# A decoder layer on one core: the first two and last three pipeline steps written out by hand, new loop orders, five idle products

## The chip, the cores and the metric

The kernel runs on 1 core of one Trainium2 chip. The metric is the device time of one execution in microseconds (us). The engines are TensorE (PE; its weight loads, PEld, overlap its products), VectorE (DVE), ScalarE (ACT), GpSimd (POOL) and SyncE (SP), which here only issues transfers (DMA). Each engine takes its own instructions strictly in the order in which they were written, and waits on semaphores for the others.

## The reference

For 32 batches of 112 tokens of width 256: a self attention without projections whose probabilities under 0.01 are cut out ("vacuum") and come back as a term with `W`, then a layer norm; a cross attention with 16 heads of 16 on 375 context rows with a mask, then a layer norm; a mixture of 8 experts of which the router takes 2 for each token, then a layer norm. Cut to what matters:

```
scores = x @ x.T / 16;  probs = softmax(scores)
vac = where(probs < 0.01, probs, 0);  sparse = where(probs < 0.01, 0, probs)
x1 = layernorm(x + (sparse / (sparse.sum() + 1e-9)) @ x + 0.01 * (vac.sum() broadcast) @ W.T)
q, k, v = x1 @ Wq + bq, ctx @ Wk + bk, ctx @ Wv + bv          # 16 heads of 16
attn = softmax(where(mask, -1e15, q @ k.T / 4));  x2 = layernorm(x1 + (attn @ v) @ Wo + bo)
p, i = top_k(softmax(x2 @ Wr), 2);  out = layernorm(x2 + sum_k p_k * (x2 @ Wi[i_k]) @ Wo[i_k])
```

## The kernel before

Each batch `b` goes through a software pipeline. One iteration `it` of a long unrolled loop works on several batches at a stage each: `Sc(it+3)` starts the self attention, `PT`, `att`, `x1T_`, `K0`, `K1` are for batch `it+2`, `V0`, `V1` for `it+1`, `scores` and `V2` for `it`, the second half of the attention (`oT`, `aT`, `Wo`) for `it-1`, and the experts for `it-2` and `it-3`. The loop runs for `it` from -5 to 35 (`FIRST`, `LAST`), and `at(b, step)` writes a step only where `b` is one of the 32 batches. So in the first and last iterations the steps that exist keep the order that the loop has for the full ones. A step writes its waits and its instruction; each engine has a loop of its own with its own order of steps.

- Self attention of a batch: `Sc` (TensorE), `self_max`, `self_nmax` (VectorE), `self_exponent` (ScalarE), `rsum`, `self_p`, `sparse`, `vacuum` (VectorE), `PT` (transpose), `sparseT` (ScalarE), `att`, `y1`, `stats1`, `mom1` (VectorE), `var1`, `rstd1` (GpSimd), `normalize_x1` (VectorE, L965), `x1T_`, `ax1T`, `qT`.
- Queries and keys are held as high and low parts and are laid by DMA into stacks of 97 partitions: `high_queries_out` and `low_queries_out` write them to memory, `stack_queries` (3 transfers a batch) reads them back, `stack_keys` moves the keys (4 pairs of 3 transfers a batch). The 97th partition of `k_stack` holds ones, which GpSimd writes once for each of 3 buffers (`fill_ones`, L495); that of `q_stack` takes the negated maxima (`neg_max_to_stack`).
- Cross attention: `scores(b, n)`, n = 0 to 15 (TensorE, L1259, 2 banks by turns), each followed by `head(b, n)` on VectorE (L861), which finds the maximum; `mx0` after head 7 and `mx1` after head 15 transpose the maxima (L1403, L1408). Then 12 blocks: ScalarE lays the mask into a bank (`lay_mask`; `lay_last` on VectorE for the last batch, L949), TensorE adds the scores (`score_block`, L1277), ScalarE takes the exponent (`exponent`, L595). `weigh_values` (L1293) multiplies by V in two octets, `o_sb`, `oT`, `rden`, `o_norm`, `aT`, `attnT`, `attn_rest`, `Wo`, `y2` and the second norm follow.
- Experts: `expert_product(e)` multiplies each expert's two matrices once in the opening (L1444), `high_expert` and `low_expert` split the result. The tokens are cut anew into 28 tiles of 128; a batch whose number is a multiple of 8 ends no tile. For a tile: `lg` (router), `cross`, `gate_max`, `gate_exp`, ... `gate`, four mixtures `m0` to `m3` (L1472, 6 products of 512 columns each) and eight steps `expert(t, e)` on VectorE (L1091), in the order of e, two for each mixture; then `stats3`, `mom3`, `var3`, `rstd3`, `normalize_out`, `store`.

The TensorE results of all but the score products share three banks G0, G1, G2; the list `USES` gives the order of their users, and `free` waits for the user before.

Of the kernel before, what the change touches and what calls it, by code (L numbers as in the profile page):

```python
# [49 lines left out]
PRODUCT_PLACE = (0, 1, 2, 4, 3, 5, 6, 7)  # L50
# [8 lines left out]
USES = [("m3", -3, "G2"), ("E6", -1, "G1"), ("x2T", -2, "G1"), ("PT", 2, "G0"), ("lg", -2, "G1"),  # L59
# [5 lines left out]
RELEASED = {"x2T": "x2_lo", "PT": "sparseT", "lg": "gate_max", "mx0": "nmaxT0", "V2": "v2", "Sc": "self_exp", "att": "y1", "V1": "v1", "V0": "v0", "aT": "attn_lo", "Wo": "y2", "K0": "k_lo0", "x1T": "ax1T", "K1": "k_lo1", "qT": "q1"}  # L65
FIRST, LAST = -5, BATCH + 3
# [7 lines left out]
         "o_sb", "oT", "rden", "o_norm", "aT", "attnT", "attn_lo", "Wo", "y2",  # L74
         "stats2", "mom2", "var2", "rstd2", "x2", "x2T", "x2_hi", "x2_lo", "lg",
         "cross", "gate_max", "gate_exp", "gate_r", "gate_p", "top_p", "top_i", "top_f", "gate_a",
         "gate", "m0", "m1", "m2", "m3", "stats3", "mom3", "var3", "rstd3",
         "out")
# [56 lines left out]
def decoder_layer(nc, x, x_T, context_T, mask, attn_w_T, wq, bq, wk, bk, wv, bv, wo, bo, wr, wi_T, wout,  # L135
                  consts, q_scratch, out):
    ctx = ExitStack()
    with ctx:  # L138
# [180 lines left out]
        def _(sp):  # L319
# [44 lines left out]
            def high_queries_out(b):  # L364
                sp.wait_ge(done["q_hi1"], b + 1)
                settle(sp)
                sp.dma_start(q_scratch[b % 2][0], q_hi[:, :, :, :].rearrange("p h c q -> p (h c q)").bitcast(fp32))\
                  .then_inc(q_hi_out[b % 2], 16)

            def low_queries_out(b):  # L370
                sp.wait_ge(done["q_lo0"], b + 1)
                settle(sp)
                sp.dma_start(q_scratch[b % 2][1], q_lo[:, :, :, :].rearrange("p h c q -> p (h c q)").bitcast(fp32))\
                  .then_inc(q_lo_out[b % 2], 16)

# [1238 lines left out]
```

## Time and profile before

| | |
|---|---|
| median of 3 runs | 764.02 us (763.23 to 766.06) |
| the profiled execution | 765.01 us, its span 763.1 us |
| TensorE busy | 731.1 us, 96% of the span, 7240 products |
| VectorE busy | 675.3 us, 88% |
| ScalarE busy | 578.7 us, 76% |
| GpSimd busy | 205.7 us, 27% |
| mean granted TensorE clock | 0.988 |

The span runs from the first to the last instruction; the time of the execution has some 2 us round it. Busy shares are means over the whole span: the opening, the repeated middle and the end have to be looked at apart.

### The profile page before, as it was taken

Reading aid. Unit: us, or ns where it says so; the run is one execution under the profiler, and the core shown is the slowest. Engines: PE = TensorE matmul, PEld = TensorE weight load, DVE = VectorE, ACT = ScalarE, POOL = GpSimd, SP = SyncE. Lnnn points to the kernel's source line nnn. Section 1 sums busy time; section 2 is a strip of 40 time slices with the busy share of each in tenths; the row PEclk is TensorE's granted clock in tenths of the full one; section 3 lists DMA queues with packets and bytes.
Section 4 is the critical chain, followed back from the end, with each engine's and each line's share of the span. In section 5 each row is a group of like instructions: output and inputs, shape, how many; then the busy total and the mean of one; then the engine's idle time right before and its main releaser. Section 6 shows DMA issues by size and latency. Waiting matters only on the chain. (4 is left out here: it accounts for less than half of the span.)

```text
span 763.1 us, 21852 instructions
## 1 busy us (share of the span) xinstructions
PE 731.1 (96%) x7240; PEld 648.6 (85%) x7240; DVE 675.3 (88%) x2608; ACT 578.7 (76%) x1435; POOL 205.7 (27%) x288
## 2 busy tenths in 40 slices
PE   5879999999999999999999999999999999999986
PEld 4768889899889988998899889988998989988764
DVE  3777799999999989999999989999999989998885
ACT  1468988787788887877888897878887798787630
POOL 4421222223323223233232322332322232321001
PEclk7999999999999999999999999999999999999997
DMA  8666764565555465555555565555545565554100
GB/s 244 184 178 181 188 169 117 150 156 147 156 146 159 125 173 133 162 151 147 154 143 147 134 184 149 148 155 143 156 132 145 160 171 144 149 136 119 33 24 20
DMA packets 75663, 110.87 MB, mean 145 GB/s; under 512 B 14224, under 2 KB 59168, under 8 KB 75552
## 3 DMA queue, kind: packets, MB, share of 16 engines
q1 hardware_dynamic: 75552, 109.49, 53.4%
q8 instruction: 58, 0.95, 0.5%
q14 instruction: 53, 0.43, 0.2%
HBM read 50.23 MB, written 18.35 MB: 90 GB/s over the span
## 5 line engine op out<-in xcount | busy, mean ns | idle before, releaser
L861 DVE CUSTOM_DVE_ANT_0 scores_left<-psum,mask_add 112x375 f32<-112x375 f32 x512 | 271.2, 540 | 27.3 <-PE psum L1259 22.3
L595 ACT ACTIVATE probsT<-psum 125x448 f32<-125x448 f32 x384 | 201.0, 542 | 32.5 <-PE psum L1277 27.4
L1259 PE MATMUL psum<-k_stack,q_stack 96*112 96x376 f32 x512 | 196.8, 388 | 6.4 <-DVE nmax L861 2.3
L580 ACT ACTIVATE psum<-mask_u 125x448 f32<-125x448 uint8 x372 | 200.2, 554 | 3.0
L1277 PE MATMUL psum<-q_stack,k_stack 97*125 97x224 f32 x768 | 143.4, 280 | 2.3 <-DVE psum L949 1.4
L1277 PEld LDWEIGHTS psum<-q_stack,k_stack 97*125 97x125 f32 x768 | 122.2, 188 | 9.4 <-ACT psum L580 3.0
L1091 DVE SCALAR_TENSOR_TENSOR late<-psum,gate,late 128x256 f32<-128x256 f32 x224 | 107.4, 479 | 17.8 <-PE psum L1472 11.5
L1259 PEld LDWEIGHTS psum<-k_stack,q_stack 96*112 96x112 f32 x512 | 90.0, 176 | 24.9 <-issue 14.0
L548 POOL TENSOR_TENSOR ctx_lo<-ctx_sb,ctx_hi 128x752 fp32r<-128x752 f32 x32 | 57.8, 1805 | 156.0 <-ACT ctx_hi L693 156.0
L1472 PE MATMUL psum<-we_hi,x_hi 128*128 128x512 f32 x224 | 90.4, 403 | 0.6 <-DVE gate_nmax L1037 0.6
L1472 PE MATMUL psum<-we_hi,x_lo 128*128 128x512 f32 x224 | 89.3, 399 | 0.0
L1472 PE MATMUL psum<-we_lo,x_hi 128*128 128x512 f32 x224 | 89.0, 397 | 0.0
L1293 PE MATMUL psum<-probsT,v_sb 125*17 125x112 f32 x3072 | 86.0, 260 | 0.7 <-ACT probsT L595 0.6
L1293 PEld LDWEIGHTS psum<-probsT,v_sb 125*17 125x17 f32 x3072 | 69.8, 97 | 14.2 <-issue 8.3
L523 POOL TENSOR_SCALAR var_eps<-moments 128x1 f32<-128x1 f32 x28 | 6.1, 218 | 207.9 <-DVE moments L961 207.9
L1472 PEld LDWEIGHTS psum<-we_hi,x_lo 128*128 128x128 f32 x224 | 42.8, 191 | 10.1
L512 POOL TENSOR_SCALAR var_eps<-moments 112x1 f32<-112x1 f32 x32 | 6.9, 215 | 161.0 <-DVE moments L936 161.0
L1472 PEld LDWEIGHTS psum<-we_hi,x_hi 128*128 128x128 f32 x224 | 43.0, 192 | 6.0 <-DVE gate_nmax L1037 0.7
L1472 PEld LDWEIGHTS psum<-we_lo,x_hi 128*128 128x128 f32 x224 | 43.2, 193 | 5.3
L703 ACT ACTIVATE attn_hi<-psum 128x224 fp32r<-128x224 f32 x32 | 11.4, 357 | 40.1 <-PE psum L1421 40.1
L861 DVE DVE_READ_ACCUMULATOR2_ANT nmax<- 112x1 f32 x512 | 41.6, 81 | 0.0
L543 POOL TENSOR_SCALAR mask_add<-mask_u 112x375 f32<-112x375 uint8 x32 | 38.7, 1208 | 3.7 <-issue 1.0
(167 smaller groups left out, 1655.0 us busy)
## 6 DMA issues: line engine op xcount, KB each, us to landing
k_stack<-k_hi SPq DMA_DIRECT2D x256, 94.0 KB, 2.2
q_stack<-q_scratch SPq DMA_DIRECT2D x96, 224.0 KB, 3.5
ctx_sb<-in_context_T SPq DMA_DIRECT2D x32, 376.0 KB, 3.4
k_stack<-k_lo SPq DMA_DIRECT2D x128, 94.0 KB, 2.2
q_scratch<-q_hi SPq DMA_DIRECT2D x32, 224.0 KB, 2.0
q_scratch<-q_lo SPq DMA_DIRECT2D x32, 224.0 KB, 2.2
xT<-in_x_T SPq DMA_DIRECT2D x32, 112.0 KB, 2.8
x_sb<-in_x SPq DMA_DIRECT2D x32, 112.0 KB, 3.3
```

The lines of the kernel that those rows point to most:

```text
L512: nc.gpsimd.tensor_scalar(var_eps[1][:, :], moments[1][:, 1:2], NEPS, None, ALU.add)\
L543: nc.gpsimd.tensor_scalar(mask_add[b % 2][:, :], mask_u8[b % MASKS][0:TOK, 0:KEYS], BIG, None, ALU.mult)\
L548: nc.gpsimd.tensor_tensor(ctx_lo[b % 2][:, :, :], ctx_sb[b % 2][:, :, :], ctx_hi[b % 2][:, :, :].bitcast(fp32), ALU.subtract)\
L580: nc.scalar.activation(psum[0:KP, ST_BANKS[i % 2], 0:4 * TOK].rearrange("p (h q) -> p h q", h=4), mask_u8[b % MASKS][:, KEYS + t * TOK:KEY ...
L595: nc.scalar.activation(probsT[:, place, i % KT, :], psum[0:KP, ST_BANKS[i % 2], 0:4 * TOK], ACT.Exp, scale=-1.0).then_inc(probs_ready, 1)
L703: nc.scalar.activation(attn_hi[:, :], bank_of["aT"][:, 0:DC * TOK], ACT.Copy).then_inc(done["attnT"], 1)
L861: nc.vector.tensor_tensor_reduce(scores_left[:, n % 2, :], psum[0:TOK, S_BANKS[n % 2], 0:KEYS], mask_add[b % 2][:, :], 1.0, 3.0e38, ALU.ad ...
L1091: nc.vector.scalar_tensor_tensor(out=mix[:, :], in0=bank_of[f"m{e // 2}"][0:ROWS, (e % 2) * DIM:(e % 2 + 1) * DIM], scalar=gates[t % 2][:, ...
L1259: nc.tensor.matmul(psum[0:TOK, S_BANKS[n % 2], 0:KEYS_EVEN], q_stack[s][0:96, pair, odd, c, :], k_stack[s][0:96, pair, c, :], start=True, ...
L1277: mm = nc.tensor.matmul(psum[0:KP, ST_BANKS[i % 2], 2 * e * TOK:2 * (e + 1) * TOK].rearrange("p (h q) -> p h q", h=2), k_stack[s][:, pair, ...
L1293: mm = nc.tensor.matmul(o_bank[32 * j:32 * j + HEAD_DIM + 1, group * TOK:(group + 1) * TOK], v_sb[b % STACKS][0:KP, t, 4 * group + j, :], ...
L1472: mm = nc.tensor.matmul(bank_of[name][0:ROWS, 0:width], x_part[:, c, :], w_part[:, c, :], start=(n == 0), stop=(n == len(parts) - 1))
```

## The change

All 32 batches go through the same computation. What differs is the order in which each engine's queue is written. The loop now covers only `it` = 2 to 28 (`FIRST_WHOLE`, `LAST_WHOLE`), in a new order on each engine; everything before and behind it is written out step by step. The banks in `USES` follow the new order. New semaphores count steps whose order against each other had been given by their places (`q_hi0`, `q_lo1`, `vac_scaled`, `sparse_r`, `gate_b`, `x1_bo`), with waits on them. GpSimd fills the ones later, and each filling has a wait of its own. Behind the last `x2T_` stand five products whose result nobody reads (`run_idle`). In the last step `m3` stands ahead of `m0`. Cut to its core (`...` marks what is left out):

```diff
-PRODUCT_PLACE = (0, 1, 2, 4, 3, 5, 6, 7)
+PRODUCT_PLACE = (0, 1, 2, 3, 4, 5, 6, 7)
...
-FIRST, LAST = -5, BATCH + 3
+FIRST_WHOLE, LAST_WHOLE = 2, BATCH - 4
...
# move_tail
+                    sp.wait_ge(done["x2"], b + 1)
...
# SP
+            load_mask(2); load_mask(3); expert_weights(0); expert_weights(1); load_x(2); expert_weights(2)
+            low_queries_out(0); high_queries_out(0); expert_weights(3); expert_weights(4); stack_queries(0, 2)
+            stack_queries(0, 0); stack_queries(0, 1); stack_keys(0, 1); stack_keys(0, 0); stack_keys(0, 2)
+            stack_keys(0, 3); load_context(2); expert_weights(5); load_x(3); stack_keys(1, 3)
...
# GpSimd
+                if k == 0:
+                    pool.wait_ge(done["mask"], 2)
+                if k == 1:
+                    pool.wait_ge(done["rstd1"], 2)
                 if k == 2:
-                    pool.wait_ge(done["rstd1"], 1)
+                    pool.wait_ge(done["rstd1"], 3)
...
+            mask(0); var1(0); rstd1(0); low_context(0); mask(1); fill_ones(0); low_context(1); var1(1)
+            rstd1(1); fill_ones(1); low_context(2); var1(2); rstd1(2); fill_ones(2); x1_bo(0); x1_bo(1)
...
# VectorE
             def sparse(b):
+                dve.wait_ge(done["self_p"], b + 1)
...
             def x_cas(b):
+                dve.wait_ge(done["vac_scaled"], b + 1)
...
             def normalize_x1(b):
                 dve.wait_ge(done["rstd1"], b + 1)
+                if b >= 2:
+                    dve.wait_ge(done["x1_bo"], b - 1)
...
+            self_max(0); self_nmax(0); rsum(0); self_p(0); vacuum(0); sparse(0); sparse_den(0); vac_scaled(0)
+            split_keys(); column_sums(); x_cas(0); sparse_r(0); y1(0); stats1(0); mom1(0); normalize_x1(0)
+            split_values(); self_max(1); self_nmax(1); rsum(1); self_p(1); sparse(1); sparse_den(1); q_lo1(0)
...
+            self_max(2); self_nmax(2); rsum(2); self_p(2); mom1(1); low_expert(3); vacuum(2); vac_scaled(2)
+            normalize_x1(1); sparse(2); head(0, 0); low_expert(4); x_cas(2); head(0, 1); head(0, 2)
...
+            head(0, 11); head(0, 12); y1(2); stats1(2); rsum(3); mom1(2); head(0, 13); head(0, 14); self_p(3)
+            vacuum(3); sparse(3); normalize_x1(2); head(0, 15); low_expert(5); head(1, 0); vac_scaled(3)
...
+            stats3(26); mom3(26); cross(27); gate_max(27); normalize_out(26); gate_r(27); gate_p(27)
+            top_p(27); top_i(27); top_f(27); gate_b(27); gate_a(27); gate(27); expert(27, 0); expert(27, 1)
+            expert(27, 2); expert(27, 3); expert(27, 4); expert(27, 5); expert(27, 6); expert(27, 7)
...
# TensorE
+            def run_idle(count):
+
+                pe.wait_ge(max_ready, HEADS * BATCH)
+                for _ in range(count):
+                    nc.tensor.matmul(psum[:, S_BANKS[0], 0:DIM * 2], we_hi[:, 0, 0:128], we_hi[:, 0, 0:DIM * 2],
+                                     start=True, stop=True, skip_group_check=True)
...
+            Sc(0); open_blocks(); sum_attn_w(); PT(0); att(0); x1T_(0); Sc(1); qT(0); PT(1); expert_product(0)
+            expert_product(1); K0(0); sum_values_bias(); att(1); K1(0); V1(0); V0(0); expert_product(2)
+            expert_product(3); Sc(2); expert_product(4); scores(0, 0); K0(1); scores(0, 1); scores(0, 2)
+            x1T_(1); K1(1); scores(0, 3); scores(0, 4); qT(1); scores(0, 5); scores(0, 6); PT(2); scores(0, 7)
...
+            score_block(31, 11); x2T_(30); weigh_values(31, 1); lg(26); oT(31); m1(26); aT(31); m0(26); Wo(31)
+            m2(26); m3(26); x2T_(31); run_idle(5); lg(27); m3(27); m0(27); m1(27); m2(27)
```

In the loops, among others: on ScalarE `self_exponent(it+3)` moves from ahead of `o_sb(it-1)` to behind it, and on VectorE `rsum`, `self_p` and `vacuum` of batch `it+3` now stand ahead of `o_norm(it-1)`.

## Rows read from the trace of the kernel before

**Rows 1.** The page: TensorE's busy time; its granted clock in 40 slices.

```profile
PE 731.1 (96%) x7240; PEld 648.6 (85%) x7240; DVE 675.3 (88%) x2608; ACT 578.7 (76%) x1435; POOL 205.7 (27%) x288
...
PEclk7999999999999999999999999999999999999997
```

**Rows 2.** Timeline of TensorE in the middle: start us, us; `mx1` of two iterations.

```profile
510.18 0.26 PE L1408 MATMUL psum<-const_sb,nmax 112*8 112x112 f32 x1
...
532.50 0.26 PE L1408 MATMUL psum<-const_sb,nmax 112*8 112x112 f32 x1
```

**Rows 3.** Stretches between two `mx1`: length, busy us of each engine, granted clock, DMA.

```profile
54.30:75.60 21.30, 19.18 (x206) 16.76 (x207) 15.24 (x58) 17.85 (x45) 4.50 (x5) 1.00 0.66 184
75.60:95.00 19.40, 19.12 (x209) 17.02 (x207) 15.38 (x61) 18.09 (x45) 5.28 (x7) 1.00 0.72 192
...
510.20:532.50 22.30, 22.30 (x229) 20.14 (x227) 21.10 (x84) 18.11 (x45) 6.35 (x9) 1.00 0.55 150
```

**Rows 4.** Timeline of TensorE in the opening, with its waits and what ended them.

```profile
16.66 3.78 PE L1444 MATMUL psum<-late 128*128 128x256 f32 x8 [1.58 <-DMA late<-in_wout]
...
31.34 0.35 PE L1385 MATMUL psum<-wv_hi,ctx_hi 128*125 128x256 f32 x1 [0.78 <-ACT self_exp L683]
...
32.86 3.69 PE L1444 MATMUL psum<-probsT 128*128 128x256 f32 x16
...
40.22 0.57 PE L1259 MATMUL psum<-k_stack,q_stack 96*112 96x376 f32 x2 [1.48 <-issue]
...
57.96 0.42 PE L1259 MATMUL psum<-k_stack,q_stack 96*112 96x376 f32 x1 [1.35 <-DMA q_stack<-q_scratch]
```

**Rows 5.** Timeline of VectorE in the opening.

```profile
11.93 0.28 DVE L818 COPY bv_wide<-bv_col 128x224 f32<-128x224 f32 x1 [1.62 <-DMA bo_row<-in_bo]
...
18.72 2.77 DVE L965 TENSOR_SCALAR x<-y,moments,rstd 112x256 f32<-112x256 f32 x1 [1.70 <-POOL rstd L506]
...
40.85 0.55 DVE L861 CUSTOM_DVE_ANT_0 scores_left<-psum,mask_add 112x375 f32<-112x375 f32 x1 [2.03 <-PE psum L1259]
```

**Rows 6.** VectorE on the tile `x`: duration ns, least, median and most.

```profile
L965 DVE TENSOR_SCALAR x<-y,moments,rstd x32: 398/403/2774, 18.7 to 684.0; 112x256 f32<-112x256 f32 x32
```

**Rows 7.** Timeline of GpSimd in the opening.

```profile
18.74 2.60 POOL L495 MEMSET k_stack<- 1x3008 f32 x1
```

**Rows 8.** Timeline of TensorE at the end, batch 31 and the last tile.

```profile
710.17 0.40 PE L1259 MATMUL psum<-k_stack,q_stack 96*112 96x376 f32 x1 [1.16 <-DVE nmax L861]
...
729.75 0.99 PE L1277 MATMUL psum<-q_stack,k_stack 97*125 97x224 f32 x4 [0.91 <-DVE psum L949]
...
736.86 1.34 PE L1293 MATMUL psum<-probsT,v_sb 125*17 125x112 f32 x48 [0.63 <-ACT probsT L595]
...
747.59 0.28 PE L1456 MATMUL psum<-wr_parts,x_hi 128*128 128x16 f32 x1 [0.87 <-DVE x_lo L1024]
...
748.81 0.80 PE L1472 MATMUL psum<-we_hi,x_hi 128*128 128x512 f32 x1 [0.62 <-DVE gate_nmax L1037]
...
754.52 0.63 PE L1472 MATMUL psum<-we_lo,x_hi 128*128 128x512 f32 x1
...
755.23 0.39 PE L1472 MATMUL psum<-we_hi,x_hi 128*128 128x512 f32 x1
...
757.07 0.39 PE L1472 MATMUL psum<-we_hi,x_lo 128*128 128x512 f32 x1
```

**Rows 9.** A stretch in the last mixture, columns as in rows 3.

```profile
750.00:752.00 2.00, 2.00 (x7) 1.52 (x6) 1.48 (x9) 0.00 (x0) 0.00 (x0) 0.50 0.19 66
```

**Rows 10.** Timeline of VectorE at the end: the last gate, the last two expert steps.

```profile
751.48 0.17 DVE L1077 TENSOR_TENSOR gate<-gate_a,gate_b 128x8 f32<-128x8 f32 x1
...
757.50 1.07 DVE L1091 SCALAR_TENSOR_TENSOR late<-psum,gate,late 128x256 f32<-128x256 f32 x2 [0.30 <-PE psum L1472]
```

**Rows 11.** Timeline of SP's queue: the first key stack issues of batches 0 and 1.

```profile
27.07 0.60 SPq L395 DMA_DIRECT2D k_stack<-k_hi  x1
...
44.26 0.51 SPq L395 DMA_DIRECT2D k_stack<-k_hi  x1
```

**Rows 12.** VectorE alone between head 0 and head 15 of batch 0.

```profile
40.85:54.21 13.36, 12.17 (x47) 1.00 0.54 156
```

More of the change, by code:

```diff
@@ new lines, in _ @@
+            nmaxT0(1); lay_mask(0, 11); high_expert(6); v1(2); exponent(0, 10); exponent(0, 11)
+            lay_mask(1, 0); v2(1); high_context(3); lay_mask(1, 1); self_exponent(4); o_sb(0)
+            for it in range(FIRST_WHOLE, LAST_WHOLE + 1):
+                at(it - 1, exponent, 0)
+                before_last(it - 1, lay_mask, 2)
+                if it == -1:
+                    high_expert(0)
+                if it == -1:
+                    high_expert(1)
+                at(it, v0)
@@ new lines, in _ @@
+            stats1(3); low_expert(6); head(1, 10); head(1, 11); head(1, 12); self_max(4); self_nmax(4)
+            head(1, 13); head(1, 14); rden(0); mom1(3); rsum(4); o_norm(0); self_p(4); head(1, 15); sparse(4)
+            vacuum(4); attn_rest(0); normalize_x1(3); y2(0); stats2(0); mom2(0); vac_scaled(4)
+            for it in range(FIRST_WHOLE, LAST_WHOLE + 1):
+                at(it, head, 0)
+                at_last(it - 1, lay_last, 7)
+                if it == 1:
+                    low_expert(5)
+                at_tile(it - 3, expert, 5)
+                if it == -2:
+                    column_sums()
+                at(it + 2, x_cas)
@@ L1116, in _ @@
[L1116 to L1119 removed]
+                if it == -2:
+                    split_values()
                 if it == -1:
@@ L1123, in _ @@
                     split_router()
+                at(it + 1, k_lo0)
+                if it == -4:
+                    split_keys()
+                at(it, head, 3)
+                at(it + 1, k_lo1)
+                at(it, head, 4)
+                at_last(it - 1, lay_last, 8)
+                at(it, head, 5)
+                at(it - 2, normalize_x2)
+                at(it + 2, sparse_den)
+                at_tile(it - 3, expert, 6)
+                at(it, head, 6)
+                at(it, head, 7)
@@ L1156, in _ @@
                 at_tile(it - 2, top_f)
-                at(it - 1, rden)
-                at(it + 2, mom1)
-                at_tile(it - 2, gate_b)
-                at(it - 1, o_norm)
-                at_tile(it - 2, gate_a)
-                at_last(it, lay_last, 2)
-                at(it, head, 13)
-                at_tile(it - 2, gate)
-                at(it + 3, rsum)
+                at(it, head, 13)
+                at(it + 3, rsum)
+                at_tile(it - 2, gate_a)
+                at(it + 3, self_p)
@@ L1187, in _ @@
+                at_last(it, lay_last, 5)
+                at(it + 3, vac_scaled)
                 at(it - 1, stats2)
+                at(it - 1, mom2)
                 at_last(it, lay_last, 6)
[L1189 to L1197 removed]
@@ new lines, in _ @@
+            stats3(22); gate_p(23); mom3(22); top_p(23); top_i(23); top_f(23); head(29, 12); gate_b(23)
+            gate_a(23); normalize_out(22); gate(23); expert(23, 0); rden(28); o_norm(28); head(29, 13)
+            expert(23, 1); mom1(31); head(29, 14); attn_rest(28); head(29, 15); expert(23, 2); expert(23, 3)
+            normalize_x1(31); y2(28); expert(23, 4); expert(23, 5); head(30, 0); stats2(28); head(30, 1)
+            mom2(28); k_lo0(31); head(30, 2); head(30, 3); normalize_x2(28); k_lo1(31); head(30, 4)
@@ new lines, in _ @@
+            head(30, 5); q_lo1(31); expert(23, 6); head(30, 6); head(30, 7); expert(23, 7); q_lo0(31)
+            x2_lo(28); head(30, 8); cross(24); gate_max(24); stats3(23); head(30, 9); head(30, 10)
+            head(30, 11); gate_r(24); gate_p(24); mom3(23); top_p(24); top_i(24); head(30, 12); top_f(24)
+            head(30, 13); head(30, 14); gate_a(24); gate_b(24); normalize_out(23); gate(24); rden(29)
+            o_norm(29); expert(24, 0); head(30, 15); expert(24, 1); attn_rest(29); expert(24, 2); head(31, 0)
```

515 lines of the change are left out of this document (308 added, 207 removed), and 20 rows, old and new, of tables (STEPS, USES).

## The prediction

> **What bounds the kernel now.** I read the page first, then stretches of the span, then each engine's timeline at the two ends. The page gives TensorE 731 us of a span of 763.1 and nearly full slices but for the first three and the last two; its clock is granted in full except in the first and the last slice [rows 1]. The repeated iteration explains the middle: from one `mx1` to the next TensorE passes in 22.32 us [rows 2], and in such a stretch it is busy for all of 22.30 us and VectorE for 21.10 [rows 3]. So the middle is TensorE's stream, with VectorE 5% behind it. Holes stand where stacks come late: 2.1 us of 21.30 in the iteration from 54.3, 0.3 of 19.40 in the next [rows 3].
>
> The ends are chains. In the opening TensorE waits 1.58 us for the first expert's weights, until 16.66; its first `scores` start at 40.22, those of batch 1 at 57.96 after a wait for `q_stack` [rows 4]. VectorE puts out `x1` of batch 0 only at 21.5, because that instruction takes 2.77 us [rows 5], where the median of its 32 is 0.40 [rows 6]; a GpSimd memset of 2.60 us runs beside it [rows 7]. At the end TensorE waits 1.16, 0.91 and 0.63 us for VectorE and ScalarE in batch 31, and then runs most of the last mixture at the low clock: 13 steps from 748.81 to 754.52 are 0.44 us each, 8 from 755.23 to 757.07 are 0.23 [rows 8], and the granted clock is 0.50 [rows 9]. After its last product there remain two expert steps, the norm and the store [rows 10].
>
> **The change part by part. Opening.** (1) VectorE no longer puts the splits of the values ahead of batch 0's softmax, and TensorE has `PT(0)`, `att(0)`, `x1T(0)`, `qT(0)` before the expert products. Counted on with the durations of before, the chain from `Sc(0)` runs to `mom1(0)` at about 11.2, waits for `mask(0)` that now stands ahead of `var1(0)` on GpSimd (about 11.5), and ends `x1(0)` near 12.9 instead of 21.5. `qT(0)` can then follow at once, as the last small weights land at 11.93 [rows 5]. The query writes leave SP at about 20.5, behind six expert transfers. (2) The keys gain nothing: `K1(0)` still follows experts 0 and 1, whose weights set 16.66 [rows 4], so SP starts on `k_stack` near 27.5 as before (27.07) and needs 12 issues of 0.6 us [rows 11]. But the query stacks no longer stand among them. Counting TensorE's stream on from `K1(0)` at 26 (`V1` and `V0` 1.5, expert products 3.69 for two [rows 4], so 5.5 for three, `Sc(2)` and its softmax 1.7) gives `scores(0, 0)` at 34.7 against 40.22; as 1.2 us of `K0(1)` and `x1T(1)` now come after it, 4.3 us are won there.
>
> (3) Part of that is lost again. `fill_ones(1)` and `fill_ones(2)` are now released by `rstd1(1)` and `rstd1(2)`, the very results for which `normalize_x1(1)` and `normalize_x1(2)` wait. Before, this happened once: memset at 18.74, `x` from 18.72, 2.77 us instead of 0.4 [rows 5 to 7]. I price each collision at the difference, 2.3 us of a standing VectorE, with the heads queued behind it: `normalize_x1(1)` ends at 37.4, head (0, 0) at 38.2 (before: 40.85 + 0.55 = 41.4 [rows 5]). The second comes at about 51 and is cut short, since VectorE reaches it late, to 1.8 us. Head 15 is then done at 53.7, before at 54.21, where the stretch of [rows 12] ends, and `scores(1, 0)` comes at 56.3 against 57.96 [rows 4], with 0.9 us of `qT(2)` done ahead of it: 2.6 us won. Lower bound of the collisions: none, as if the 2.77 us had another cause (opening 4 us better); upper: two full ones (0.5 us worse).
>
> The Trainium skill ("SBUF — State Buffer", section on who interferes with whom) says that a `tensor_scalar` that can use VectorE's second port is blocked for the whole of a GpSimd instruction that began first. The pair of rows above agrees with it, and by it both collisions come; without it the sum would be 752.
>
> (4) Batch 1's key stacks start after `k_lo1(1)`, near 41.8 instead of 44.26 [rows 11]. So the 2.1 us of holes in the stretch from 54.3 and the 0.3 of the next [rows 3] should close: 2.4 us. Opening in all: −5.0, between −9 (no collision, all holes closed) and 0 (VectorE sets the pace from head 0 on).
>
> **Loops.** Every iteration does the same work on each engine. I laid the new TensorE order along the steps between starts of before (a mixture is 6 × 0.23 [rows 8]) and the other queues beside it. VectorE, 18.8 us of it from head 0 on in my count, stays ahead at every score; ScalarE, some 18 us, too; SP's 12 key issues end 2 us before their first user. The tightest places are `oT` after `o_sb` (0.25 us spare) and `aT` after `o_norm` (0.7 us). I take 0. The number of short transposes next to score products changes by a few per iteration; a neighbour changes a step by under 0.1 us, so ±0.1 us an iteration, ±2.4 over the 24 of this kind. The added waits (`sparse` for `self_p`, `x_cas` for `vac_scaled`, `gate` for `gate_b`, `move_tail` for `x2`) are on results that are older than the waiting instruction in the new order. Behind `move_tail` on SP stand key and query stacks, but `x2(it-2)` is long done by then. `normalize_x1` waits for `x1_bo` of two batches earlier: done too. All cost nothing; bound from above, 0.2 us for each adjacent pair in the last step, 0.4 us.
>
> **Last three steps.** Of the three waits shown, 2.7 us [rows 8], I take 1.5 back: the new order puts `lay_last` blocks and heads of batch 31 before mixture steps that the old loop put between them. Bounds: 0 and 4 (the view has three more such waits of 0.3 to 0.7 us).
>
> **Idle products and the final mixture.** Now TensorE ends `x2T` near 746.7, does `lg` from 747.59, waits for `gate_max` and starts `m0` at 748.81 [rows 8]: with 0.87 and 0.62 us of pauses the granted clock goes to 0.50, its low level, 1.2 GHz [rows 9]. The five products of 512 columns at 0.23 us [rows 8] make 1.15 us and fill that hole; `lg` waits at most 0.1 us for them. `m3` comes first now and takes a bank that `lg` doesn't hold, so it follows `lg` at 748.3 without the 0.6 us wait. At full clock: `m3` to 749.7, `m0` 751.1, `m1` 752.5, `m2` after the first two expert steps (gate done at 751.65 as before [rows 10], two steps of 0.54): 752.8 to 754.4. But the expert steps run in the order 0 to 7, so four of them, not two, remain after the last product: 754.4 + 4 × 0.54 = 756.6, against 758.58 now [rows 10]. Gain 2.0. If the clock falls all the same, each mixture takes 6 × 0.43 = 2.56 us, the last product ends near 758.7 and the four steps at 760.9: 2.3 worse than now.
>
> **Sum.** −5.0 + 0 − 1.5 − 2.0 = −8.5 from the profiled run of 765.01 us: 756.5. That run lies 1.0 above the median of the three (764.02, from 763.23 to 766.06), so against the median I say 756.0.
>
> **Rivals.** (a) No collisions with the memset: for it, only one such pair stands in the trace; against it, 32 instructions of this line and only that one is as long [rows 6]. 752; chance 0.18. (b) The clock falls in the end anyway, since the transposes and `lg` round the idle products are thin: 756.0 + 4.3 = 760.3; chance 0.10. (c) The opening gives nothing, because from head 0 on VectorE is the pace (it is busy for 12.17 of the 13.36 us between head 0 and head 15 before [rows 12]): 761.0; chance 0.10. (d) Slower: in the loop `self_exponent` now stands after `o_sb` on ScalarE, and `rsum`, `self_p` and `vacuum` stand before `o_norm` on VectorE. If that makes `o_norm` later than its 0.7 us of spare, `aT`, and TensorE behind it, wait in each of the 24 whole iterations. It decides from 0.5 us of wait on (24 × 0.5 = 12 us eats the 8.5): with 0.5, 768; chance 0.06. Against it: the same wait now is hidden in a stream that is never idle [rows 3]. (e) It does not do what it says: TensorE's stream is the time, the chains at the ends only move, 763; chance 0.08. The likeliest keeps 0.48, with a range of its own from 753 to 759.
>
> **How the numbers follow.** 756.0. The range 749.5 to 761.5 takes in (a), (b) and (c) and leaves out (d) and (e) and what lies beyond the bounds, some 0.2. About 0.5% (3.8 us) is what a measurement of this kernel can tell from no change. Faster by more than that (under 760.2): the likeliest, (a), half of (b) and a little of the rest, 0.80. Same: the other half of (b), most of (c) and (e), 0.13. Slower: (d) and a little beyond, 0.07.
>
> **What would show it.** Right: `x1` of batch 0 out near 13; first `scores` near 34.7; two long `x` instructions beside memsets; `mx1` to `mx1` still 22.3 us in the middle; clock 1.00 through the last mixture and four expert steps behind it. Wrong: waits of `aT` or `oT` in every iteration, a first score later than 38, a last mixture at steps of 0.43 us, or mean iterations that differ by over 0.1 us.

## The result, and where the time went

The changed kernel takes **780.07 us** (median of 5 runs, 778.01 to 784.41), the kernel before 764.02 (762.64 to 766.06, 5 runs). The ratio is **1.019, 95% interval 1.016 to 1.022** (these two medians alone give 1.021). I had predicted 756.0 with a range of 749.5 to 761.5 and a chance of 0.07 for slower. The change is slower.

The profiled run of the changed kernel is the longest of its five: 784.41 us, span 782.6. In the kernel without the idle products, whose order is the same up to the last step, `mx1(28)` starts 4.4 us earlier than in this one (681.8 for 686.1), so about four of its 19.5 us above the span before are this one execution's, three of them ahead of `mx1(3)`. One of the twelve executions of e4 took 890.85 us at a granted clock of 0.749 and is left out of its ratio.

The page of the changed kernel, lines as in [rows 1]:

```profile
PE 737.4 (94%) x7245; PEld 659.0 (84%) x7245; DVE 689.1 (88%) x2608; ACT 592.5 (76%) x1435; POOL 199.6 (25%) x288
...
PEclk8899999999999999999999999999999999999999
```

TensorE and VectorE are busy for 6 and 14 us more with the same work, five products apart. So VectorE's instructions got longer on average (TensorE's busy time includes the modelled ends of its products and says less). The next table cuts each span at the starts of `mx1`, as the timeline of TensorE gives them; it has the experiments too, to which the sections below refer. TensorE's first product, `Sc(0)`, waits for the constants and started between 3.67 us (e5) and 4.68 us (e10). So that this doesn't count, the first column is shifted in each run to the 3.88 us of the kernel before; the other columns are as read. One profile stands for each kernel, and the opening of one and the same order differs by some us between profiles (the changed kernel and e8: 124.6 and 121.6).

| kernel (us) | start of `mx1(3)`, shifted | `mx1(3)` to `mx1(28)` | `mx1(28)` to the end | whole-tile iteration |
|---|---|---|---|---|
| before | 115.7 | 547.1 | 100.3 | 22.3 |
| changed | 124.6 | 561.5 | 96.5 | 22.9 |
| e1 short ctx_lo | 120.4 | 542.8 | 96.4 | 22.2 |
| e2 memsets in front | 115.0 | 560.4 | 96.4 | 22.9 |
| e3 gate_p on ScalarE | 122.1 | 544.3 | 98.0 | 22.2 |
| e4 before, idle products | 115.9 | 547.7 | 98.8 | 22.3 |
| e5 e2 and e3 | 113.1 | 544.4 | 99.6 | 22.2 |
| e6 high_context back | 120.2 | 567.6 | 98.0 | 22.9 |
| e7 before, high_context moved | 114.5 | 564.9 | 100.5 | 23.1 |
| e8 no idle products | 121.6 | 560.2 | 96.4 | 22.9 |
| e10 e5, low_context(0) later | 113.7 | 544.9 | 99.5 | 22.2 |
| e11 head 12 first | 122.8 | 556.8 | 96.4 | 22.7 |
| e12 e10, scores twice | 114.7 | 545.1 | 96.9 | 22.2 |

So of the 19.5 us, 8.9 are lost ahead of `mx1(3)`, 14.4 in the loop, and 3.8 are won at the end.

**The loop.** The timeline of TensorE of the changed kernel, the rows that answer to [rows 2], with the one pause between them:

```profile
553.05 0.26 PE L1548 MATMUL psum<-const_sb,nmax 112*8 112x112 f32 x1
...
571.84 0.42 PE L1398 MATMUL psum<-k_stack,q_stack 96*112 96x376 f32 x1 [0.45 <-DVE nmax L943]
...
575.94 0.26 PE L1548 MATMUL psum<-const_sb,nmax 112*8 112x112 f32 x1
```

The pitch, from one `mx1` to the next, is 22.89 us for 22.32. At 571.84 a score product stands for 0.45 us until VectorE's maximum of head 12 (`nmax`) frees its bank; the next iteration has the same pause (0.49 at 594.77). Eighteen iterations of this kind account for 10.2 of the 14.4 us; the rest lies in the seven others between `mx1(3)` and `mx1(28)`, whose waits I didn't follow one by one. One step back, on VectorE and then on GpSimd:

```profile
569.07 1.35 DVE L1136 TENSOR_SCALAR gate_p<-gate_exp,gate_r 128x8 f32<-128x8 f32 x1
...
571.23 0.55 DVE L943 CUSTOM_DVE_ANT_0 scores_left<-psum,mask_add 112x375 f32<-112x375 f32 x1
```

```profile
568.59 1.79 POOL L587 TENSOR_TENSOR ctx_lo<-ctx_sb,ctx_hi 128x752 fp32r<-128x752 f32 x1 [2.37 <-ACT ctx_hi L743]
```

`gate_p`, eight numbers in a row, takes 1.35 us and ends just when GpSimd's `ctx_lo` does (568.59 + 1.79 = 570.38; 569.07 + 1.35 = 570.42). `ctx_lo` is the low part of the context, made by `low_context` from what ScalarE's `high_context` puts out. In the kernel before it took 0.23 us. There `ctx_lo` starts at 526.87 and meets another instruction of that size, `top_f`. These are its GpSimd and VectorE timelines:

```profile
526.87 1.81 POOL L548 TENSOR_TENSOR ctx_lo<-ctx_sb,ctx_hi 128x752 fp32r<-128x752 f32 x1 [2.71 <-ACT ctx_hi L693]
```

```profile
527.47 1.24 DVE L1062 CAST top_f<-top_i 128x8 f32<-128x8 uint32 x1
```

So the kernel before has such a collision in each iteration too, but at a place where head 12 is done and head 13 has room, and TensorE doesn't stand [rows 3]. The changed kernel issues `high_context` earlier on ScalarE (ahead of `lay_mask(it, 0)`), and has moved the gate's steps and heads on VectorE: the same collision now falls in front of head 12.

**The opening.** VectorE's timeline, to set against [rows 5]:

```profile
13.85 1.85 DVE L1053 TENSOR_SCALAR x<-y,moments,rstd 112x256 f32<-112x256 f32 x1 [1.69 <-POOL rstd L546]
...
18.34 1.48 DVE L963 TENSOR_SCALAR self_p<-self_exp,self_rsum 112x112 f32<-112x112 f32 x1
...
21.28 2.27 DVE L907 TENSOR_TENSOR wo_lo<-wo_sb,wo_hi 128x512 fp32r<-128x512 f32 x1
...
38.82 2.78 DVE L1053 TENSOR_SCALAR x<-y,moments,rstd 112x256 f32<-112x256 f32 x1
...
58.92 0.71 DVE L1053 TENSOR_SCALAR x<-y,moments,rstd 112x256 f32<-112x256 f32 x1 [2.94 <-POOL x_bo L576]
```

and GpSimd's:

```profile
13.78 1.77 POOL L587 TENSOR_TENSOR ctx_lo<-ctx_sb,ctx_hi 128x752 fp32r<-128x752 f32 x1
...
17.14 2.61 POOL L535 MEMSET k_stack<- 1x3008 f32 x1
...
21.24 1.77 POOL L587 TENSOR_TENSOR ctx_lo<-ctx_sb,ctx_hi 128x752 fp32r<-128x752 f32 x1 [1.49 <-ACT ctx_hi L743]
...
38.84 2.60 POOL L535 MEMSET k_stack<- 1x3008 f32 x1
...
55.36 2.65 POOL L535 MEMSET k_stack<- 1x3008 f32 x1
58.09 1.40 POOL L576 TENSOR_TENSOR x_bo<-x,bo_row 112x256 f32<-112x256 f32 x2
```

Each of the four long VectorE instructions runs beside a GpSimd one and ends 0.1 to 0.2 us behind it, the subtraction 0.5 us. The last is another thing: VectorE stands for 2.94 us ahead of `normalize_x1(2)` until `x1_bo(0)` has read the buffer that it writes, and `x1_bo(0)` is queued on GpSimd behind `fill_ones(2)`. VectorE was free for it at 55.98, so the memset, which ran until 58.01, would have met it in any case. TensorE shows what these cost (compare [rows 4]):

```profile
15.76 0.63 PE L1460 MATMUL psum<-const_sb,x 112*128 112x112 f32 x2 [4.92 <-DVE x L1053]
...
20.20 0.44 PE L1449 MATMUL psum<-const_sb,sparse 112*112 112x112 f32 x1 [1.25 <-DVE sparse L968]
20.43 3.65 PE L1584 MATMUL psum<-late 128*128 128x256 f32 x8
...
38.87 0.52 PE L1398 MATMUL psum<-k_stack,q_stack 96*112 96x376 f32 x1
...
42.40 0.40 PE L1398 MATMUL psum<-k_stack,q_stack 96*112 96x376 f32 x1 [1.80 <-DVE nmax L943]
...
60.16 0.26 PE L1548 MATMUL psum<-const_sb,nmax 112*8 112x112 f32 x1 [3.12 <-DVE nmax L943]
```

The expert products start at 20.43 instead of 16.66: they stand behind the chain to `x1(0)` and behind `PT(1)`, which waits 1.25 us for `sparse` of batch 1, late by the collision of `self_p(1)` with `fill_ones(0)` (1.48 us for 0.27). Scores of batch 0 start at 38.87 instead of 40.22; then VectorE is late for the maxima, and `mx1(0)` comes at 60.16, 5.9 us later than before (54.27; in e8's profile, with the same opening, 58.38).

**The end.** TensorE's timeline, its granted clock by stretches, and VectorE's last expert steps, against [rows 8 to 10]:

```profile
767.62 1.40 PE L1593 MATMUL psum<-we_hi 128*128 128x512 f32 x5
768.85 0.17 PE L1603 MATMUL psum<-wr_parts,x_hi 128*128 128x16 f32 x1
...
774.10 0.51 PE L1619 MATMUL psum<-we_hi,x_hi 128*128 128x512 f32 x1 [0.50 <-DVE late L1182]
...
775.37 0.40 PE L1619 MATMUL psum<-we_hi,x_lo 128*128 128x512 f32 x1
```

```profile
772.00:774.00 2.00, 1.60 (x7) 0.96 (x6) 1.66 (x6) 0.00 (x0) 0.00 (x0) 1.00 0.09 30
```

```profile
775.80 2.25 DVE L1182 SCALAR_TENSOR_TENSOR late<-psum,gate,late 128x256 f32<-128x256 f32 x4 [0.58 <-PE psum L1619]
```

From `lg` to the end of the last expert step it takes 778.05 − 768.85 = 9.2 us, before 758.58 − 747.59 = 11.0: the 1.8 us (2.0 predicted), the clock of 1.00, and the four steps behind the last product are as predicted.

### The profile page after: what moved, and what is told of

The parts are those of the page before. It is cut to its first block and busy times, and to the rows that moved or that the text cites. A ratio compares the mean times of both kernels' runs of the same rounds, so it can differ in the third digit from the quotient of the medians.

```text
span 782.6 us, 22204 instructions
## 1 busy us (share of the span) xinstructions
PE 737.4 (94%) x7245; PEld 659.0 (84%) x7245; DVE 689.1 (88%) x2608; ACT 592.5 (76%) x1435; POOL 199.6 (25%) x288
## 5 line engine op out<-in xcount | busy, mean ns | idle before, releaser
L1398 PE MATMUL psum<-k_stack,q_stack 96*112 96x376 f32 x512 | 185.9, 367 | 16.5 <-DVE nmax L943 14.4
L1416 PE MATMUL psum<-q_stack,k_stack 97*125 97x224 f32 x768 | 150.0, 280 | 0.1
L1416 PEld LDWEIGHTS psum<-q_stack,k_stack 97*125 97x125 f32 x768 | 137.1, 189 | 10.8 <-DVE psum L1035 1.1
L1478 PE MATMUL psum<-x1T,wq_sb 128*128 128x112 f32 x256 | 35.4, 284 | 0.0
```

The lines of the kernel that those rows point to most:

```text
L1398: nc.tensor.matmul(psum[0:TOK, S_BANKS[n % 2], 0:KEYS_EVEN], q_stack[s][0:96, pair, odd, c, :], k_stack[s][0:96, pair, c, :], start=True, ...
L1416: mm = nc.tensor.matmul(psum[0:KP, ST_BANKS[i % 2], 2 * e * TOK:2 * (e + 1) * TOK].rearrange("p (h q) -> p h q", h=2), k_stack[s][:, pair, ...
L1478: mm = nc.tensor.matmul(bank_of["qT"][:, r * TOK:(r + 1) * TOK], wq_sb[:, c, r * 128:(r + 1) * 128], x1T[:, c, :], start=(c == 0), stop=(c ...
```

## Experiments

Ratios are to the kernel before on the same chip, where its medians were 764.9 to 766.5 us; so a time just under 764.02 can be a gain. The theory from here on, A: VectorE instructions of some kinds stand still while GpSimd runs `ctx_lo` or a memset, and the change has put those moments in front of maxima for which TensorE waits. The rival, B: the new order itself costs, by neighbours on TensorE or by `o_sb` and `o_norm` late for `oT` and `aT` (my rival (d)).

**e1, e2, e3: take away one collision, leave the order.**

```diff
 e1 (also: ctx_lo zeroed once at the start)
-    ctx_lo[b % 2][:, :, :], ctx_sb[b % 2][:, :, :], ctx_hi[b % 2][:, :, :].bitcast(fp32), ALU.subtract)
+    ctx_lo[b % 2][:, :, 0:8], ctx_sb[b % 2][:, :, 0:8], ctx_hi[b % 2][:, :, 0:8].bitcast(fp32), ALU.subtract)
 e2
+    fill_ones(0); fill_ones(1); fill_ones(2)      # their waits on mask and rstd1 go
     mask(0); var1(0); rstd1(0); low_context(0); mask(1); low_context(1); ...
 e3 (ScalarE; at_tile(it - 2, gate_p) goes from VectorE's loop)
     at(it + 1, v1)
+    at_tile(it - 2, gate_p_act)                   # activation Copy, scale=gate_recip
```

> The changed kernel with GpSimd's subtraction ctx_lo (L587) over 8 of its 376 columns, the rest of ctx_lo being zero from a memset at the start: most of the low part of the context is left out of the products' values, and the number of products stays. The order of every engine is that of the changed kernel. Theory A (the subtraction of 1.79 us holds up VectorE's gate_p, 1.35 us for 0.23, and with it the maxima of heads 12 and 13 and TensorE's next scores, in every iteration): the pitch of the iterations with a whole tile falls from 22.90 to 22.3 us, some 11 us over the loop, and the opening, which loses its two collisions with ctx_lo (wo_lo 2.27 us, normalize_x1(0) 1.85 us), gives 0 to 2 us more: 766 to 770 us, ratio to the kernel before 1.003 to 1.008. Theory B (the new neighbours of products on TensorE, or o_sb and o_norm late for oT and aT): the pitch stays at 22.8 or above, ratio 1.015 to 1.02.

> The changed kernel with its three memsets fill_ones at the front of GpSimd's queue, so that they collide with nothing of VectorE's and x_bo(0) has none of them ahead. Theory A (the three memsets of 2.6 us cost self_p(1), normalize_x1(1) and, over the wait on x_bo(0), mx1(0)): mx1(0) starts at 54 to 57 instead of 60.16 and the whole is 3 to 6 us shorter than the changed kernel, ratio to the kernel before 1.011 to 1.015. Against: mask(0), var1(0) and rstd1(0) may come up to 8 us later behind them, by which x1(0) is late and the queries start at 24 instead of 20.4; then the gain is 0 to 2 us, or a loss. Theory B (the opening is bound by VectorE's maxima and TensorE's own rows): within 1 us of the changed kernel.

> The changed kernel with gate_p of the loop's tiles (the 128x8 gate probabilities, exponentials times the reciprocal) done by ScalarE behind v1 instead of by VectorE between the maxima of heads 12 and 13. Theory A (gate_p is the instruction that ctx_lo holds up): the wait of 0.45 us ahead of scores 14 goes, the pitch falls from 22.90 to 22.4 us, 8 to 11 us less than the changed kernel, ratio 1.005 to 1.01. Theory A': ctx_lo then holds up the next VectorE instruction that it can, and the pitch stays at 22.7 or above. Theory B (neighbours, or o_sb and o_norm): nothing changes, ratio 1.015 to 1.02; ScalarE has one instruction more of about 0.2 us in each iteration, which makes self_exponent and o_sb later and the pitch, if B's second half is right, longer.

Measured: e1 761.54 us, 0.994 (0.992 to 0.996); e2 773.61, 1.011 (1.008 to 1.013); e3 763.88, 0.997 (0.996 to 0.999). The loop fell to 542.8 us in e1 and to 544.4 in e3, 17 to 19 us below the changed kernel and below the 547.1 of the kernel before: more than I expected of either (766 to 770 us; 8 to 11 us less). e3 settles the loop: one 128x8 instruction moved to another engine, everything else in its order, gives back 0.7 us of pitch. Its VectorE timeline has nothing long ahead of head 12 (the last row), though `ctx_lo` is there (553.04 to 554.83):

```profile
553.12 0.15 DVE L1140 RECIPROCAL gate_r<-gate_sum 128x1 f32<-128x1 f32 x1
553.19 0.41 DVE L1016 BATCH_NORM_STATS2 stats<-y 112x6 f32<-112x256 f32 x1
554.03 0.17 DVE L1150 MAX8 top_p<-gate_p 128x8 f32<-128x8 f32 x1 [0.43 <-ACT gate_p L773]
554.12 0.14 DVE L962 TENSOR_SCALAR self_nmax<-self_top 112x1 f32<-112x1 f32 x1
554.35 0.09 DVE L1155 MATCH_VALUE_LOAD top_i<-top_p,gate_p 128x8 f32 x1
554.43 0.16 DVE L1155 FIND_INDEX8 top_i<-top_p,gate_p 128x8 uint32<-128x8 f32 x1
554.52 0.18 DVE L1021 BATCH_NORM_AGGREGATE moments<-stats 112x2 f32<-112x6 f32 x1
554.71 0.55 DVE L951 CUSTOM_DVE_ANT_0 scores_left<-psum,mask_add 112x375 f32<-112x375 f32 x1
```

All of these run at their usual length beside `ctx_lo` (the maximum overlaps it for 0.12 us only; others that lie wholly within it take 0.54 to 0.55 too, as at 77.38 in the changed kernel). So e3 works because no instruction of the kind that stands still is left in that stretch (`self_nmax` is a TENSOR_SCALAR too, but of one value a row, and isn't held up). And since the pitch is 22.15 both here and in e1, where `gate_p` stays on VectorE, and 22.31 before, the new order by itself costs nothing: B is refuted. Whether the 0.16 us below the kernel before are the order's own gain, or what the collision in the kernel before costs it, is open: no run takes that one away.

e2 puts `mx1(0)` at 54.2 (shifted as in the table), as expected, and `mx1(3)` at 115.0 for 124.6, or for 121.6 in e8. By the times the memsets cost 6.5 us (780.07 for 773.61).

**e6, e7: move `high_context` alone.** If A holds, a move of one ScalarE instruction must move the collision.

```diff
 e6, the changed kernel                     e7, the kernel before
     at_tile(it - 2, gate_exp)                  at(it, v2)
-    at(it + 2, high_context)              +    at(it + 2, high_context)
     before_last(it, lay_mask, 0)               before_last(it, lay_mask, 0)
     ...                                        ...
     at(it - 1, o_sb)                           at(it - 1, o_sb)
+    at(it + 2, high_context)              -    at(it + 2, high_context)
```

> The changed kernel with ScalarE's high_context of the loop put back behind o_sb, where the kernel before has it. GpSimd's ctx_lo, which waits for it, then starts some 1.7 us later, at about 570.3 in the iteration read at 568.6, when gate_p (at 569.1) has ended. Theory A: gate_p takes 0.23 us again; what is then hit is top_f, the 128x8 conversion in front of head 13, at about 570.5, which would wait until ctx_lo ends at 572.1 and make head 13 late instead of head 12. So the pitch falls only if head 13 has more room than head 12: 22.3 to 22.9, and in the trace the long instruction is top_f (0.9 to 1.5 us) and not gate_p. Theory B (ctx_lo has no part in it): gate_p stays at 1.35 us wherever ctx_lo is.

> The kernel before with one thing changed: ScalarE's high_context of the loop ahead of lay_mask(it, 0), the place that it has in the changed kernel. GpSimd's ctx_lo then starts at about 524.8 instead of 526.9 in the iteration read. Theory A: it holds up gate_p (at 525.8, 0.23 us) and what follows it ahead of head 12 by about 1 us, and the pitch rises from 22.3 by 0.2 to 0.7 us, ratio 1.005 to 1.02; top_f takes 0.2 instead of 1.24 us. If the kernel before has room ahead of head 12, or theory B (the new order of VectorE or TensorE is what costs) holds, the pitch stays at 22.3 and the ratio within 0.998 to 1.002.

Measured: e6 789.39 us, 1.033 (1.029 to 1.036); e7 782.43, 1.025 (1.021 to 1.029). e7 makes a slowdown of this size out of the kernel before by one moved line. The direction was as A said, the victim was not: `ctx_lo` came 0.2 us ahead of `x_cas`, behind which head 11 is queued. The VectorE and GpSimd timelines of e7:

```profile
559.91 2.03 DVE L909 SCALAR_TENSOR_TENSOR x_cas<-w_sum,vac_scaled,x_sb 112x256 f32<-112x256 f32 x1
```

```profile
559.70 1.96 POOL L548 TENSOR_TENSOR ctx_lo<-ctx_sb,ctx_hi 128x752 fp32r<-128x752 f32 x1 [0.51 <-ACT ctx_hi L693]
```

The loss is larger than I had expected of e7 (at most 1.02). In e6 the victim is `gate_a`, behind head 13 (I had said `top_f`, which got away by 0.2 us): the pitch stays at 22.9, and the iterations without a whole tile get longer. VectorE, and what TensorE waits for in that kernel's loop:

```profile
570.45 1.47 DVE L1155 TENSOR_SCALAR gate_a<-const_sb,top_f,top_p 128x8 f32<-128x8 f32 x1
571.84 0.27 DVE L963 TENSOR_SCALAR self_p<-self_exp,self_rsum 112x112 f32<-112x112 f32 x1
572.02 0.49 DVE L1161 TENSOR_SCALAR gate_b<-const_sb,top_f,top_p 128x8 f32<-128x8 f32 x1
```

```profile
573.28 0.41 PE L1561 MATMUL psum<-const_sb,o_norm 112*128 112x112 f32 x2 [0.53 <-DVE o_norm L1100]
```

This is the very wait of my rival (d), `aT` for `o_norm`, and it comes when `ctx_lo` strikes ahead of `o_norm`. In the changed kernel no such pause stands in the iterations of 22.9 us; one of 0.59 us stands in one of its short ones, at 641.04.

**e11: the order alone, on VectorE.**

```diff
     at(it + 2, stats1)
+    at(it, head, 12)
     at_tile(it - 2, gate_p)
     ...
     at(it + 2, mom1)
-    at(it, head, 12)
```

> The changed kernel with VectorE's head(it, 12) of the loop ahead of gate_p instead of behind the gate's three steps; nothing else, and no work moved to another engine. Scores 12 are done at about 569.9 in the iteration read, so head 12 ends at 570.4, about when ctx_lo ends (570.40). Theory A (what costs is that maxima are queued behind an instruction that ctx_lo holds up): gate_p then takes 0.23 us, TensorE's wait of 0.45 us for nmax ahead of scores 14 goes, the pitch falls from 22.9 to 22.3 to 22.6, 6 to 11 us less than the changed kernel, ratio 1.005 to 1.011. Against: head 13 then stands behind the whole of the gate's steps (0.9 us) and is as late as before, so that the wait is only moved to scores 15: pitch 22.8 to 22.9, ratio 1.017 to 1.02.

Measured: 779.10 us, 1.018 (1.015 to 1.021), pitch 22.7. The pause of 0.45 us for `nmax` is gone, and only 0.2 us of the 0.7 came back. I expected more. The ratio is that of "against", but the wait didn't move to scores 15: set beside e3, TensorE's stream falls back first at a mixture, by 0.3 us, and by 0.2 us more behind it. VectorE, ScalarE and TensorE there:

```profile
587.48 0.50 DVE L1136 TENSOR_SCALAR gate_p<-gate_exp,gate_r 128x8 f32<-128x8 f32 x1
588.21 0.14 DVE L954 TENSOR_SCALAR self_nmax<-self_top 112x1 f32<-112x1 f32 x1
```

```profile
588.38 0.35 ACT L733 ACTIVATE self_exp<-psum,self_nmax 112x112 f32<-112x112 f32 x1 [1.26 <-DVE self_nmax L954]
```

```profile
588.88 0.50 PE L1619 MATMUL psum<-we_hi,x_hi 128*128 128x512 f32 x1 [0.15 <-ACT self_exp L733]
```

`self_nmax` is now queued behind head 12 and `gate_p`, both of which wait for scores 12; ScalarE waits for it, and the mixture for the bank that ScalarE's exponent frees. `gate_p` takes 0.50 us for 0.23 though it begins just after `ctx_lo` has ended. So this reordering was a poor cure; taking the instruction off VectorE was a good one.

**e4, e8: the idle products.** e4 is the kernel before with `run_idle(5)` ahead of the last `lg` (products of 512 columns; 128, as I wrote below, is the width of their weights), e8 the changed kernel without it.

```diff
 e4                                         e8
+    if it == BATCH + 1:                   -    x2T_(31); run_idle(5); lg(27)
+        run_idle(5)                       +    x2T_(31); lg(27)
     at_tile(it - 2, lg)
```

> The kernel before with nothing changed but five idle products of 128 columns ahead of the last lg. Theory A (the granted clock falls to 0.50 in the last mixture because TensorE had paused at the last logits; the idle products keep it at 1.00): the mixture's products of the last tile take 1 to 2 us less, 762 to 763 us, ratio 0.996 to 0.999. Rival: the clock falls anyway, or the products are only in the way: ratio 1.000 to 1.001.

> The changed kernel without the five idle products ahead of the last lg. Theory A (they hold the granted clock at 1.00): it falls to 0.50 for some 4 us within the last mixture, and from the last lg to the end of the span it takes 15 us instead of 13.5, 1 to 2 us more than the changed kernel, ratio 1.020 to 1.022. Rival: with the new order of the last steps TensorE pauses less before the last logits, so that the clock stays at 1.00 without them: the same time or 0.3 us less, ratio 1.018 to 1.019.

Measured: e4 765.65 us, 1.000 (0.998 to 1.002); e8 780.33, 1.021 (1.017 to 1.025). In the stretch of [rows 9] and the one behind it, the granted clock of e4:

```profile
750.00:752.00 2.00, 2.00 (x10) 1.64 (x9) 1.56 (x9) 0.00 (x0) 0.00 (x0) 1.00 0.19 66
752.00:754.00 2.00, 0.99 (x5) 0.50 (x4) 1.66 (x6) 0.00 (x0) 0.00 (x0) 1.00 0.00 0
```

and of e8, behind its last `lg`:

```profile
766.00:768.00 2.00, 2.00 (x10) 1.64 (x9) 1.58 (x9) 0.00 (x0) 0.00 (x0) 1.00 0.19 66
768.00:770.00 2.00, 1.47 (x7) 0.91 (x6) 1.59 (x6) 0.00 (x0) 0.00 (x0) 1.00 0.00 0
```

So in the old order the idle products do hold the clock at its high level, and the stretch from `mx1(28)` is 1.5 us shorter in the profile; the times, with an interval of ±0.2%, neither show nor exclude it. In the new order they do nothing in these profiles: the clock stays at 1.00 without them, and the end takes 96.4 us for 96.5. The time of e8 doesn't decide this by itself: its 1.021 lies where I had put A, but its interval holds the rival's 1.018 too, and 780.33 us are the changed kernel's 780.07. The 1.8 us that I gave to the idle products came with the new order of the last steps.

**e5, e10, e12: a version that beats both.** e5 has e2 and e3 together. e10 adds `mask(1)` ahead of `low_context(0)` on GpSimd. e12 adds to that a second issue of five score products of batch 31.

```diff
 e10
-    mask(0); var1(0); rstd1(0); low_context(0); mask(1); low_context(1); var1(1)
+    mask(0); var1(0); rstd1(0); mask(1); low_context(0); low_context(1); var1(1)
 e12, in scores(b, n)
+    if b == BATCH - 1 and 8 <= n <= 12:
+        nc.tensor.matmul(...)                     # the same product, same bank
     nc.tensor.matmul(...).then_inc(scores_ready, 1)
```

> The changed kernel with the fill_ones memsets in front and gate_p of the loop's tiles on ScalarE, both at once. Theory A (two separate collisions of GpSimd with VectorE, one in the opening and one in each iteration): the gains of the two add up. The opening as with the memsets in front (mx1(0) at 54.2), the pitch 22.2 as with gate_p on ScalarE, the end 1 us shorter for the idle products: 764 minus 7 = 757 us, ratio 0.985 to 0.992. If the first gain only filled time that the second needs, the ratio is 0.995 or above.

> The kernel with both changes (memsets in front, gate_p of the loop on ScalarE) and one more: GpSimd's mask(1) ahead of low_context(0), so that ctx_lo(0) no longer starts together with normalize_x1(0), which took 1.85 us there for 0.40. Theory A (x1(0) sets the first queries and with them the first scores): x1(0) is done at 13.9 instead of 15.3, the first scores start 1 to 1.4 us earlier than 37.4, and the whole is 1 to 1.4 us shorter, 757 us, ratio 0.988 to 0.991. Against: ctx_lo(0) then falls on split_values, whose conversion (0.41 us) or subtraction (0.86 us) waits up to 1.5 us, and with it self_p(1) and the expert weights: nothing gained or 1 us lost, ratio 0.990 to 0.993.

> The kernel with memsets in front, gate_p on ScalarE and mask(1) ahead of low_context(0), and one more: the score products of heads 8 to 12 of batch 31 are issued twice into the same bank (the second overwrites the first with the same values). In the profile without this, TensorE is busy for 4.35 of the 5 us from 710, the granted clock falls to 0.50 from about 715 to 720, and the step from mx1(30) to mx1(31) takes 20.4 us; in the profiles of the changed kernel, where the clock stays at 1.00 there, 17.3. Theory (the small pauses there let the clock fall, and more work in them holds it): 17.3 to 18.3 us for that step, and the whole 1.5 to 3 us shorter, ratio 0.984 to 0.987. Rival: the clock falls all the same, or five more products of 0.17 us are only in the way: ratio 0.988 to 0.990.

Measured: e5 758.39 us, 0.991 (0.988 to 0.994); e10 757.17, 0.988 (0.986 to 0.991); e12 757.89, 0.990 (0.988 to 0.993). The two cures add up (0.991 against 0.997 and 1.011), and all three beat both kernels; among themselves they can't be told apart. In e10 the first scores start at 36.85 (e5: 37.41, both shifted as in the table), and `normalize_x1(0)` takes 0.41 us. e12's ratio is the one that I had given to the rival.

Something else showed in e5. Its end takes 99.6 us and not 96.5: the granted clock falls in batch 31. It does in the profiles of e3, e6 and e10 too.

```profile
711.00:712.00 1.00, 0.74 (x13) 0.47 (x16) 1.00 (x5) 0.70 (x2) 0.23 (x1) 0.91 0.00 0
712.00:713.00 1.00, 1.00 (x31) 1.00 (x24) 1.00 (x3) 0.00 (x0) 0.00 (x0) 0.50 0.02 4
```

Before it fell, TensorE had small pauses of 0.22 and 0.26 us for `nmax` (708.90 and 711.35), as it has in the profile of e8 (0.21, 0.16 and 0.19), where it doesn't fall. Nor does it in the kernel before, where the pause ahead of 710.17 is 1.16 us [rows 8]. So the length of a single pause doesn't tell; what does is open. With e12's five products more, the clock stays at 1.00 in this profile and the step from `mx1(30)` to `mx1(31)` takes 17.8 us for the 20.4 of e10, as expected; the median does not show it. In how many of the executions of either the clock falls there is open.

## Why the prediction was wrong, step by step

- **Loops, "I take 0": the step that failed.** I bounded it by the neighbours on TensorE, ±2.4 us; it measured +14.4, because `gate_p` stood still beside `ctx_lo` (1.35 us for 0.23) and the maximum of head 12, and TensorE behind it, came late in every whole-tile iteration. I counted VectorE's work at the durations of before, and these depend on what GpSimd does at the moment. I had named the mechanism for the opening (step 3) and didn't ask where `ctx_lo`, 1.8 us in each of the 32 batches, would fall. The rows were at hand: `top_f` at 527.47 took 1.24 us for 128x8 values. The effect that I did bound is small: the pitch without the collision is 0.16 us below the one before (e1, e3). I also counted 24 whole iterations, where 18 have this pitch in the stretch measured.
- **Rival (d), 768, chance 0.06.** Right side, and a loss in each iteration of about the size that I named (0.57 us for 0.5), but not its mechanism: in these iterations `aT` doesn't wait. So it is luck that the 0.5 fits. e6 shows what it takes to make it wait.
- **Opening, (1): `x1(0)` near 12.9.** It ended at 15.7: 1.45 us is a collision with `ctx_lo(0)` that I hadn't counted, the rest is `mask(0)`, which waits for its transfer until 11.65 and ended at 12.85 instead of 11.5. **(2)** `K1(0)` at 26 "whose weights set 16.66": no longer; the expert products stand behind `x1T(0)`, `qT(0)` and `PT(1)` in the new order and started at 20.43, and `K1(0)` came at 28.9. I also left `K1(0)`'s own 1.4 us out of the sum. So the first scores came at 38.87, not at 34.7; with the memsets in front and `mask(1)` moved (e10; `wo_lo` still takes 2.20 us there) at 36.85. **(3)** Of the two collisions with `fill_ones` that I counted, the first was priced well (2.78 us for 0.40 at 38.82, 2.4 for my 2.3); a third, of `fill_ones(0)` with `self_p(1)`, I had missed; the second turned into the wait for `x1_bo(0)`, which I had put down as "done too". That was wrong: it stood behind the memset in GpSimd's queue. As for the Trainium skill's rule that I cited ("SBUF — State Buffer", who interferes with whom), the trace agrees with it that VectorE stands still at every one of these places; which began first the rows can't always tell (at 38.82 and in [rows 5] and [rows 7] VectorE's start is recorded 0.02 us ahead of the memset's). I applied it to the memsets only. **(4)** That the holes after `mx1(0)` close, 2.4 us, isn't shown: from `mx1(0)` to `mx1(3)` the opening of before takes 60.1 to 61.5 us (before, e4, e7), the new one 62.4 to 64.4 with the memsets where the change has them and 59.4 to 60.9 with them in front (e2, e5, e10, e12). In all, the opening measured +8.9 in the profile (+5.9 in e8's), where I had −5.0; with both cures (e5) it is −2.6.
- **Last three steps and the end, −3.5.** Measured −3.8 from `mx1(28)` to the end of the span, of which 1.8 behind the last `lg` (2.0 predicted) and 2.0 ahead of it (1.5 predicted). Right in both; but in e8's profile the same comes without the idle products, so they had no part in it.

e5 shows what the order is worth with the two cures, which themselves move work: −2.6 − 2.7 − 0.7 = −6.0 us, counted as in the table (−6.2 in the spans), where I had said −8.5 for the change. The change lost that, and 16 us more, to the moments at which GpSimd runs.

## What to carry over

Before moving anything, list GpSimd's long instructions and mark on VectorE's timeline which instruction starts within them: those durations are not properties of the instruction, and a sum made of them can break when either engine is reordered, even through a third (here ScalarE's `high_context`). Look for one whose duration is far above its size, as a 128x8 conversion of 1.24 us: it is a collision that happens to be hidden, and the next reordering may uncover it. What worked here: the long memsets at the start of GpSimd's queue (6.5 us), and the small instruction that stood still moved to ScalarE (16 us). Whether the kernel before would gain by either is untested.

## What the runs showed of the hardware

- Which VectorE instructions stand still until the GpSimd instruction has ended: `TENSOR_SCALAR` of 128x8 (1.35 for 0.23 us; 1.47 for 0.27), 112x112 (1.48 for 0.27) and 112x256 values (1.85 and 2.78 for 0.40), the conversion of 128x8 (1.24 for 0.17), the subtraction `wo_lo` of two 128x512 operands (2.27 us, 0.69 in the kernel before), and `SCALAR_TENSOR_TENSOR` `x_cas` (2.03 for 0.48). What runs beside it at its usual length: the maxima from TensorE's accumulation memory (0.55), `TENSOR_SCALAR` of one value a row (0.14), `RECIPROCAL` (0.15), `BATCH_NORM_STATS2` (0.41), `MAX8` (0.17), `FIND_INDEX8` (0.16). Those that stand still end with the GpSimd instruction or up to 0.5 us behind it, whatever their size, so that in ratio the smallest pay most. The Trainium skill ("SBUF — State Buffer", section on who interferes with whom) names two kinds: those that use VectorE's second port, and those with two SBUF inputs while GpSimd reads; `x_cas` and `wo_lo` are of the second, and the trace agrees. `gate`, which has two such inputs too, takes its usual 0.15 us where it begins 0.01 us ahead of `ctx_lo` (704.87 in the changed kernel).
- In the other direction GpSimd lost little where it was seen: `ctx_lo` takes 1.96 us in e7 for 1.81, begun 0.12 us after a `TENSOR_SCALAR` of VectorE.
- In batch 31 the granted clock fell to 0.50 after pauses of 0.22 and 0.26 us (e5) and held at 1.00 with pauses of 0.21, 0.16 and 0.19 (e8) and with one of 1.16 (the kernel before).
